# First stage of a four-layer graph network: loops unrolled, masks turned between node tiles, features stored unscaled, and a quarter of the node norms on GpSimd

## What is computed

```python
def _L0_gnn_ref(x, adj, W, a, node_weights, node_bias, ln_gamma, ln_beta):
    x = x * node_weights[None, :, None] + node_bias[None, :, None] + x
    h = jnp.einsum('bnf,fo->bno', x, W)
    mu = jnp.mean(h, axis=-1, keepdims=True)
    var = jnp.mean((h - mu) ** 2, axis=-1, keepdims=True)
    h = (h - mu) * jax.lax.rsqrt(var + LN_EPS) * ln_gamma + ln_beta
    residual = h
    s1, s2 = h @ a1, h @ a2
    e = leaky_relu(s1[:, :, None] + s2[:, None, :], 0.2)
    attention = softmax(where(adj[None, :, :] > 0, e, NEG_INF), axis=-1)
    h_prime = jnp.einsum('bij,bjo->bio', attention, h) + residual
    return jax.nn.elu(h_prime)
```

## Time and profile before

| | before |
|---|---|
| median of three runs | 3704.32 us |
| the profiled execution | 3706.8 us |
| its span (first to last instruction) | 3705.0 us |
| PE busy | 3456.8 us, 93% |
| VectorE busy | 3098.7 us, 84% |
| ScalarE busy | 1736.4 us, 47% |
| GpSimd busy | 1778.2 us, 48% |
| mean granted clock of TensorE | 0.965 |
| first stage | 0 to about 203.8 us of the span |
| layer 0's attention | about 203.8 to 688 us |

### The profile page before, as it was taken

One profiled execution on the slowest core, in us unless ns is written; L12 is line 12 of the kernel. 1 busy time (PEld: TensorE's weight loads), 2 busy tenths in 40 slices (PEclk: granted clock), 3 DMA queues, 4 the chain that ended last, 5 costly groups with the idle time before them and its releaser, 6 DMA issues. The chain is left out here.

```text
span 3705.0 us, 59650 instructions
## 1 busy us (share of the span) xinstructions
PE 3456.8 (93%) x21147; PEld 1823.0 (49%) x21147; DVE 3098.7 (84%) x7016; ACT 1736.4 (47%) x3578; POOL 1778.2 (48%) x832
## 2 busy tenths in 40 slices
PE   5679999678999999999999999999997999699999
PEld 4579999542111111111111111111116999699999
DVE  6878888577999999999999999999956776477777
ACT  7821111355666666666666666666662444300100
POOL 2400000113888888888888888888890111000000
PEclk8789999888999999999999999999997999899999
DMA  6522121473001110010001111011003332211220
GB/s 237 199 98 87 52 86 58 149 252 116 24 11 28 28 28 15 19 30 28 28 5 28 28 28 28 7 28 28 5 5 104 115 115 81 115 47 61 84 83 27
DMA packets 80079, 240.72 MB, mean 65 GB/s; under 512 B 13616, under 2 KB 40624, under 8 KB 65584
## 3 DMA queue, kind: packets, MB, share of 16 engines
q1 hardware_dynamic: 79792, 236.92, 18.9%
HBM read 151.80 MB, written 85.07 MB: 64 GB/s over the span
## 5 line engine op out<-in xcount | busy, mean ns | idle before, releaser
L1472 POOL TENSOR_TENSOR a_w<-a_w,keep_mask_t 128x1024 f32<-128x1024 f32 x768 | 1627.4, 2145 | 301.1 <-ACT a_w L1457 301.1
L1457 ACT ACTIVATE a_w<-a_sc_ps 128x512 f32<-128x512 f32 x2048 | 1111.4, 595 | 718.1 <-PE a_sc_ps L1379 716.4
L1412 DVE CUSTOM_DVE_ANT_0 a_mx_ps<-a_mx_ps,a_mbias 128x512 f32<-128x512 f32 x1992 | 1310.5, 718 | 74.0 <-PE a_mx_ps L1341 73.2
L1357 PE MATMUL a_o_ps<-a_w,a_v 128*33 128x512 f32 x4096 | 1081.0, 606 | 6.0 <-POOL a_w L1472 5.8
L868 PE MATMUL g_acc<-g_hv,g_w 128*128 128x129 f32 x8192 | 923.6, 276 | 43.2 <-ACT g_hv L825 32.3
L868 PEld LDWEIGHTS g_acc<-g_hv,g_w 128*128 128x128 f32 x8192 | 922.1, 193 | 44.9 <-DVE g_w L804 44.9
L804 DVE SCALAR_TENSOR_TENSOR g_w<-g_row,keep_s,keep_mask_t 128x1024 f32<-128x1024 f32 x512 | 647.1, 1282 | 201.9 <-PE g_acc L868 185.0
L1379 PE MATMUL a_sc_ps<-a_qs,a_ks 97*128 97x512 f16 x2048 | 621.9, 385 | 0.3
L1425 DVE TENSOR_TENSOR a_w<-a_w,keep_mask_t 128x1024 f32<-128x1024 f32 x256 | 457.7, 1788 | 34.0 <-ACT a_w L1457 28.6
L1341 PEld LDWEIGHTS a_mx_ps<-a_ks,a_qs 32*128 32x128 f16 x1992 | 88.9, 91 | 789.3 <-DVE a_mx L1412 427.9
L1341 PE MATMUL a_mx_ps<-a_ks,a_qs 32*128 32x512 f16 x1992 | 376.6, 385 | 7.5 <-DVEq L1429 7.5
(11 more groups left out here) (237 smaller groups left out, 2237.5 us busy)
## 6 DMA issues: line engine op xcount, KB each, us to landing
h_nodes<-p_h SPq DMA_DIRECT2D x16, 1032.0 KB, 3.9
g_h<-h_nodes SPq DMA_DIRECT2D x16, 1032.0 KB, 7.4
p_adj_in<-in_adj SPq DMA_DIRECT2D x16, 1024.0 KB, 8.3
g_row<-u_rows SPq DMA_DIRECT2D x32, 512.0 KB, 7.3
v<-p_v SPq DMA_DIRECT2D x32, 264.0 KB, 3.0
a_v<-v SPq DMA_DIRECT2D x16, 528.0 KB, 3.6
p_x<-in_x SPq DMA_DIRECT2D x8, 1024.0 KB, 5.0
mask_bias<-p_mbias SPq DMA_DIRECT2D x16, 512.0 KB, 8.9
```

What stands on the lines that cost most here:

```text
L1357: mm = nc.tensor.matmul(o_ps[2 * HD * a:2 * HD * a + HD + 1, c % 2, :], v[u][:, jt, a, :], w[:, g % PB, a, :], start=(jt == 0), stop=(jt = ...
L1412: last = nc.vector.tensor_tensor_reduce(out=mx_ps[:, buf, a, :], in0=mx_ps[:, buf, a, :], in1=mbias[:, t, kc * BANK:(kc + 1) * BANK], scal ...
L1457: nc.scalar.activation(w[:, g % PB, a], sc_ps[:, n % SB], ACT.Exp, scale=SCALE).then_inc(exp_done, 1)
L1472: nc.gpsimd.tensor_tensor(w[:, g % PB], w[:, g % PB], keep["mask_t"][:, jt, c * BANK:(c + 1) * BANK].unsqueeze(1).to_broadcast([P, 2, BANK ...
```

## The change

- `masks_and_nodes0` has no loops: eight turns are written out for each engine.
- The masks of batch b are made and turned in turn b, between the node tiles: PE turns the first after the third node group and the second after the fourth; ScalarE keeps them there, VectorE makes them at the start and in the middle of its turn.
- The last quarter of the norms of x (four node tiles) goes to GpSimd (`norm_last`): four scale-and-shift instructions of 128x128 and one maximum of 128x512. rstd_x and shift_x are doubled.
- The features are stored as they come out of the projection (`store_h0`, into the DRAM array v, 130 columns a tile with both score columns). `norm_h`, `affine` and GpSimd's L385 are gone. The stored inverse root is kept for each batch, and keep_v = s2_02 x root is one product on GpSimd at the end.
- The seven weight loads are issued by ScalarE at its start. VectorE begins with the split of the node bias, which waits for them, and makes no mask before turn 0.
- In g0 ScalarE scales the raw features twice (by keep_v for hv, by the root in place for the residual), and VectorE multiplies by gamma (`scale_y`) and adds twice beta (`shift_y`) in every half; `FIN` is (6, 8, 10, 12, 14) there and (10,) in g3.

The diff, cut to its core:

```diff
+def feature_lines(io, b):
+    return io["v"][bass.ds(b, 1)].rearrange("one g p n -> one (g p n)").rearrange("one (p n) -> p (one n)", p=P)[:, 0:T * (F + 2)]
...
-        rstd_x, shift_x = s.sb("rstd_x", [P, T]), s.sb("shift_x", [P, T])
+        rstd_x, shift_x = s.sb("rstd_x", [P, 2, T]), s.sb("shift_x", [P, 2, T])
...
+            def store_h0(b, k):
+                sp.wait_ge(h0_kept, TH * (b + 1) + 2)
+                sp.dma_start(feature_lines(io, b), flat(h0[k][:])).then_inc(h0_stored[k], 16)
+            def turn(b, k):
+                if b > 0:
+                    store_h0(b - 1, 1 - k)
+                sp.wait_ge(m01_ready, 2 * b + 1)
+                if b < B - 1:
+                    load_adj(b + 1, 0)
+                store_mbias(b, 0)
+                sp.wait_ge(m01_ready, 2 * b + 2)
+                if b < B - 1:
+                    load_adj(b + 1, 1)
+                store_mbias(b, 1)
+                if b < B - 3:
+                    sp.wait_ge(x_normed, (CH - 1) * (b + 2))
+                    sp.wait_ge(last_normed, b + 2)
                     load_x(b + 3, 1 - k)
...
         def _(pool):
+            def norm_last(b, k):
+                pool.wait_ge(chain_x, (b + 1) * CHAIN)
+                if b >= 2:
+                    pool.wait_ge(h_turned, CH * (b - 1))
+                for t in range(T - T // CH, T):
+                    ins = nc.gpsimd.tensor_scalar(hn[k][:, t, :], x[k][:, t, :], rstd_x[:, k, t:t + 1], shift_x[:, k, t:t + 1],
+                                                  ALU.mult, ALU.add)
+                ins.then_inc(last_scaled, 1)
+                pool.wait_ge(last_scaled, b + 1)
+                quarter = hn[k][:, T - T // CH:T, :]
+                nc.gpsimd.tensor_scalar(quarter, quarter, 0.0, None, ALU.max).then_inc(last_normed, 1)
+            def turn(b):
+                if b < B - 1:
+                    norm_last(b + 1, (b + 1) % 2)
+                if b > 0:
                     root_h(b - 1)
-                if not late(b):
+                if b < B - 2:
                     root_x(b + 2)
...
+            nc.gpsimd.tensor_tensor(keep["v"][:], keep["s2_02"][:], keep["u"][:], ALU.mult).then_inc(value_scaled, 1)
...
         def _(dve):
+            def turn(b, k):
+                mask(b, 0)
+                if b < B - 1:
+                    shift_of_x(b + 1)
+                if b > 0:
                     stats_h(b - 1, 1 - k)
+                mask(b, 1)
+                if b < B - 2:
+                    stats_x(b + 2, k)
+                if b > 0:
                     scores(b - 1, 1 - k)
+            split_nb()
+            stats_x(0, 0)
+            spread_nb()
             shift_of_x(0)
             prepare()
+            stats_x(1, 1)
+            for b in range(B):
+                turn(b, b % 2)
             stats_h(B - 1, 1)
             scores(B - 1, 1)
             fs.vector(nc, dve, keep)
-            affine(B - 2)
             fs.vector_rows(nc, dve)
-            affine(B - 1)
...
         def _(act):
-            def norm_h(b, k):
...
+            def turn(b, k):
                 def ahead(q):
-                    if not last(b):
+                    if b < B - 1 and q < CH - 1:
                         norm_x(b + 1, 1 - k, q)
+                if b > 1:
                     act.wait_ge(scores_kept, 2 * (b - 1))
+                    act.wait_ge(h0_stored[k], 16 * (b // 2))
                 keep_hT(b, 0)
                 keep_hT(b, 1)
                 ahead(0)
                 keep_h0(b, k, 0)
                 keep_h0(b, k, 1)
                 keep_hT(b, 2)
                 ahead(1)
+                keep_mask(b, 0)
                 keep_h0(b, k, 2)
+                keep_h0(b, k, 3)
                 keep_hT(b, 3)
                 ahead(2)
+                if b < B - 1:
+                    keep_mask(b, 1)
                 keep_h0(b, k, 4)
                 keep_h0(b, k, 5)
...
         def _(pe):
+            def turn(b, k):
                 turn_nodes(b, k, 0)
                 turn_nodes(b, k, 1)
                 project(b, 0)
                 project(b, 1)
                 turn_nodes(b, k, 2)
+                turn_mask(b, 0)
                 project(b, 2)
+                project(b, 3)
                 turn_nodes(b, k, 3)
+                if b < B - 1:
+                    turn_mask(b, 1)
                 project(b, 4)
                 project(b, 5)
...
-    FIN = (10, 12, 14)
+    FIN = (6, 8, 10, 12, 14) if residual_elu else (10,)
...
+            def scale_y(n):
+                dve.wait_ge(affine_loaded, 32)
+                dve.wait_ge(drained, n + 1 + 2)
+                nc.vector.tensor_tensor(y[:], y[:], gamma[:].unsqueeze(1).to_broadcast([P, IT, F]), ALU.mult).then_inc(gamma_done, 1)
+            def shift_y(n):
+                dve.wait_ge(gamma_done, n + 1)
+                nc.vector.scalar_tensor_tensor(out=y[:], in0=beta[:].unsqueeze(1).to_broadcast([P, IT, F]), scalar=2.0, in1=y[:],
+                                               op0=ALU.mult, op1=ALU.add).then_inc(y_ready, 1)
...
             def scale_h(b, k, loads):
+                if residual_elu:
+                    nc.scalar.copy(value[:, k:k + 1, :], keep["v"][:, bass.ds(b, 1), :]).then_inc(value_kept, 1)
+                    nc.scalar.copy(hv[:, k, :, F], keep["s2_02"][:, bass.ds(b, 1), :].rearrange("p one t -> p (one t)"))
+                    nc.scalar.copy(rstd[:, k:k + 1, :], keep["u"][:, bass.ds(b, 1), :]).then_inc(value_kept, 1)
+                    act.wait_ge(value_kept, 2 * b + 2)
...
                 act.wait_ge(h_loaded[k], 16 * loads)
                 for t in range(T):
+                    last = nc.scalar.activation(hv[:, k, t, 0:width], h[:, k, t, 0:width], ACT.Copy, scale=value[:, k, t:t + 1])
+                if residual_elu:
+                    act.wait_ge(h_scaled, 4 * b + 4)
+                    for t in range(T):
+                        last = nc.scalar.activation(h[:, k, t, 0:F], h[:, k, t, 0:F], ACT.Copy, scale=rstd[:, k, t:t + 1])
+                    last.then_inc(h_normed, 1)
             def exp_y(n):
-                act.wait_ge(drained, n + 1 + 2)
+                act.wait_ge(y_ready, n + 1)
```

More of the change, by code:

```diff
@@ L258, in masks_and_nodes0 @@
         CHAIN_H = 5
-        def batches(eng, turn):
-            turn(0, 0, 0)
-            with eng.Fori(0, B // 2 - 2) as i:
-                turn(2 * i + 1, 1, i)
-                turn(2 * i + 2, 0, i + 1)
-            for b in range(B - 3, B):
-                turn(b, b % 2, b // 2)
-        def last(b):
-            return isinstance(b, int) and b == B - 1
-        def first(b):
-            return isinstance(b, int) and b == 0
-        def late(b):
-            return isinstance(b, int) and b >= B - 2
         def rstd(b):
-            return rstd_last[:] if last(b) else rstd_h[:]
-        def scaled(b):
-            return hn[0] if last(b) else h1
+            return keep["u"][:, b, :]
         @block.sync
@@ L378, in _ @@
             root_x(0)
+            norm_last(0, 0)
             root_x(1)
[L380 removed]
+            for b in range(B):
+                turn(b)
             root_h(B - 1)
[L382 to L385 removed]
+            pool.wait_ge(rooted_h, B)
+            pool.wait_ge(fs.factors, 3)
+            nc.gpsimd.tensor_tensor(keep["v"][:], keep["s2_02"][:], keep["u"][:], ALU.mult).then_inc(value_scaled, 1)
         @block.vector
@@ L582, in turn @@
                 keep_h0(b, k, 5)
-                if last(b):
-                    norm_h(b - 1, 1 - k)
-                else:
-                    keep_mask(b, 1)
-                    if not first(b):
-                        norm_h(b - 1, 1 - k)
             act.sem_inc(mt_kept, 2)
@@ L634, in project @@
                 mm.then_inc(projected, 1)
-            def turn(b, k, half):
+            def turn(b, k):
                 turn_nodes(b, k, 0)
@@ L661, in _ @@
             pe.wait_ge(nb_ready, 1)
-            batches(pe, turn)
+            for b in range(B):
+                turn(b, b % 2)
+            turn_mask(B - 1, 1)
             fs.tensor(nc, pe, keep)
```

204 lines of the change are left out of this document (72 added, 132 removed).

## The result

The changed kernel takes **3662.3 us** in the median (3660.6 to 3664.9) against 3704.5: 0.9886 of before, 95% interval 0.9869 to 0.9903. Forecast was 3666, range 3654 to 3682. The profiled execution lasted 3660.6 us, with a span of 3658.7 against 3705.0. The total was met; its terms were not.

What follows compares the result with a forecast made beforehand. ScalarE was taken to bound the first stage's turn, PE the attention stage. Start -0.6, body -30.6, tail -9.4, factor copies -0.4 and attention +2.5 sum to -38.5 us: 3665.8, said as 3666, range 3654 to 3682.

Steps and rivals of the forecast that it cites:

- range's lower end, 3654: Whole kernel: weights landing early (W = 8, 3660, chance 0.11) with a first-stage turn of 14.2 (-6).
- ScalarE sets the turn.: First stage: ScalarE, busy 19.2 of a 20.7 us turn, bounds it; removing 4.79 of scaling and 1.64 of norms leaves 13.5.
- The masks' order: First stage: masks between a batch's own node tiles fill PE's gaps but leave PE in ScalarE's loop; no gain of their own.
- The turn after, 14.8: First stage, turns 1 to 6: 13.5 us of ScalarE work and 1.3 of waits for PE; ends 14.2 and 16.
- Turns 0 and 7: First stage's end turns: turn 0 21.4 us long with nothing prepared, turn 7 11.0 without norms.
- Start: Before PE's first node matmul: it starts at 26.5 (19 to 28.5) instead of 27.15, -0.6 us.
- W = 15: Start: time in us when all seven weight loads have landed; bounded by about 8 and 17.2.
- Tail: Last feature copy to next stage's first load: 15.5 us against 24.9, -9.4 (bounds 12.5 to 18).
- The blocked product, -2.95: First stage's tail: VectorE's 16x16 product, 3.13 us and ending with GpSimd's L385, falls to 0.2.
- Queue rival: First-stage turn: 5.25 MB need 14.1 us at 372 GB/s, 17 with late loads; 0.22 together with PE as bound.
- +2.5 at the end: Attention stage's end: two more dependent steps before the exponential, +2.5 us.
- the 0 in the loop: Attention loop: VectorE's two extra instructions a half batch stay under PE's 28.6 us; cost 0 (to +1 a half batch).

Runs made afterwards that it cites:

- a_pad24: Changed kernel with 24 more TensorE instructions (12 transposes of the identity) ahead of the first stage; 3651.8 us, 0.9855 of before.
- b_no_features: Kernel before with feature scaling, gamma and beta left out but for one tile of 16; 3693.7 us, 0.9963 of before.
- b_both: Kernel before with masks turned between node tiles and feature scaling, gamma and beta out but for one tile of 16; 3684.3 us, 0.9937.
- a_masks_end: Changed kernel with 24 added TensorE instructions and both masks turned at the turn's end again, copied by ScalarE next turn; 3679.8 us, 0.9928.
- a_no_bias: Changed kernel with VectorE's mask bias computed on 16 of 2048 columns only; 3660.3 us, 0.9870 of before.
- a_port: Changed kernel with 24 added TensorE instructions and GpSimd's 128x2048 product put back behind the last root; 3658.9 us, 0.9865.
- b_unroll: Kernel before with only the first stage's turns written out instead of looped, on all engines; 3714.2 us, 1.0016 of before.

## Why the prediction was right, and where it was not

- **Total.** Right, and by luck: two misses cancel. The first stage gained 13 us more than forecast, the attention stage lost 13 more. Without the stop in the attention stage the kernel takes 3651.8 us (a_pad24), below the range. The range's lower end, 3654, also rests on a slip: it takes 6 us off 3660 for a turn of 14.2, but six turns of 0.6 less are 3.6.
- **"ScalarE sets the turn."** It was 0.93 busy, but the step "4.79 us are removed, so the turn loses them" was wrong. Scaling, gamma and beta removed with nothing else changed are 1.1 us a turn (b_no_features). The prediction had read the pieces: PE's low clock after ScalarE's scaling, and 17.8 us of ScalarE's waits for PE. It did not ask what would stand in the place of the scaling if only that went. The masks' order, priced at zero, is shown to carry a part of the gain (b_both, a_masks_end). For the second rstd_x buffer, also at zero, the row at 117.94 speaks, but it was not tried by itself.
- **The turn after, 14.8; measured 13.4.** Two terms. ScalarE's 13.5 was a sum of group times; instructions in a row overlap by about 0.1 us each, and its busy time is 12.25. The 1.3 us of waits for PE did not come: between 46 and 126 us ScalarE waits for VectorE's shift alone, 6.7 us in five waits. PE's full clock in these turns fits that; it was not tried apart. The bound is VectorE (busy 13.58; forecast 13.3 busy, "close behind"), as a_no_bias shows for two thirds of what was taken from it.
- **Turns 0 and 7.** 20.3 from PE's start to 46.0, and 9.0; forecast 21.4 and 11.0.
- **Start.** W = 15 was right to 0.1 us; PE started 0.7 earlier than said.
- **Tail.** 14.7 for 15.5, but by two errors: last copy to root 4.4 for 2.5 (VectorE waited 2.06 us for the root before it, which had begun 0.16 us into a mask and took 4.53 us, and only then made its scores and all the statistics), and the last store to the next stage 2.0 for 4.4: it is now the store of the factors, where before it was one of a batch's features. That its size makes the difference is argued, not tried. The blocked product, -2.95, was right, and a_port bears out its cause.
- **Queue rival.** It put 14.1 us a turn on 5.25 MB at 372 GB/s. The engines moved 358 to 403 in the four turns from 58.28 on, 389 on average, at a share of about 1.00, and VectorE's waits for adjacency were 0.3 at most: not the bound, though near it.
- **Attention.** The +2.5 at the end and the 0 in the loop were right, as a_pad24 shows (+2.1 in all). The missing term is the stop behind the jump back and the clock it costs, +13.5 us. It comes from writing out the first stage's loops (b_unroll): code of another stage, off every engine's timeline.

## What to carry to other kernels

An engine that is 93% busy is the bound only if the rest of its turn would not grow when work is taken from it; look at who is queued behind whom at the point where the work stood, and price the order and the buffers together with the work. A change that alters only how long one engine's program is can move time in a stage far behind it: look for a wait named "issue" a few records into each iteration but the first, and try the same kernel with some tens of instructions more ahead of it. Here that brought the changed kernel from 3662 to 3652 us.

## What the runs showed that was not expected

- TensorE stopped for 1.8 to 2.3 us, five records into every iteration of a loop but the first, when the loop began at place 184 of 256 by my count, and for 4.4 to 5.1 us in one piece when it began at 196; it did not at 36, 124 or 208.
- Behind such a stop, so close to the wait at the jump (1.7 to 2.2 us), the granted clock was 0.65 to 0.79 over the following 8 to 9 us in all three iterations. Behind a wait at the jump alone it was 1.00 in most (after 1.67 and 2.29 us) and 0.79 to 0.81 in some (after 1.94 and 2.17 us).
- A mask on VectorE that began 0.2 us ahead of a root on GpSimd held it: 4.5 to 4.6 us instead of 2.9 to 3.2. A root that began 0.17 us ahead of a mask did not hold the mask.
- The DMA engines carried 400 GB/s at a share of 1.02 in a turn, more than the 372 that a share of 0.72 at 268 GB/s lets one expect.
